# A block-inverse recurrence beside a gated network on one core: 16x16 diagonal blocks with one link, the visit of the values moved, two columns interleaved

## The chip, the cores and the metric

The kernel runs on one core of one Trainium2 chip. The metric is the device time of one execution in microseconds. The kernel before takes 1741.5 us (median of 3 runs, 1741.11 to 1744.32).

## The reference, cut to what matters

A block of a network for 4 sequences of 2048 tokens with 256 features, all in fp32. First an attention-like recurrence with 4 heads of 64, in chunks of 64 tokens, then a gated network of three hidden layers of 1024.

```python
h = layernorm(x) * (1 + ca) + sa
v = h @ Ww.T;  rk = unit(h per head);  wk = rk shifted by one token
A0 = -where(strict, (wk @ wk.T) * L, 0)          # 64x64 per chunk and head
A = inv(eye - A0)
intra = where(strict, (rk @ wk.T) * L, 0)
for each chunk:                                  # 32 in sequence
    v_new = A @ v - (A @ wk) @ S
    o = rk_g @ S + intra @ v_new
    S = gamma_C * S + wk_g @ v_new
x = x + ga * (h + (alpha * o) @ Wr.T)
h = layernorm(x) * (1 + cb) + sb
g = silu(h @ w1.T * s1) * (h @ w2.T * s2)        # 256 -> 1024, the gated layer, l1
g = gelu(g @ h1.T * s)                           # l2
g = gelu(g @ h2.T * s)                           # l3
x = x + gb * (g @ w3.T * s3)                     # y, the last layer
```

## The kernel before, in words

There are 32 steps, one for each chunk of 64 tokens of all 4 sequences. The hidden activations of the network lie with features on the partitions and 256 tokens as columns. Each is kept as two parts, `act_hi` (rounded to fp32r) and `act_lo` (the rest), so each product of a 128x128 weight block is two matmuls of 256 columns, about 114 ns each. A step has 8 columns of `l1` (8 matmuls each), of `l2` and of `l3` (16 each), and the last layer `y` (32).

The steps are woven. In pass n of the steady state (`mixed`) TensorE does, for step n-1, `l3` and `y`; for step n, `l1` and `l2`; between these columns stand the parts of the recurrence for step n, and, for step n+1 and n+2, what does not depend on the state (the letter `ahead` in the lists). The order is written out by hand in the lists `alone` (step 0), `opening` and `second` (step 1), `third` (step 2) and `mixed` (steps 3 to 33, 24 of them in a loop of two passes of 12). Every engine walks the same list in order and does its own share of each item (`part` in each engine's block), so an item's place fixes its place in five queues at once. There is no other planner.

The inverse of the 64x64 lower triangular matrix is built for 8 pairs of (half of the heads, q) in both halves of the partitions:

- `gram` gives the products; GpSimd masks them to `near` (inside a diagonal block of `SB`), `cross` (between such blocks inside a half of 32) and `far` (between the two halves).
- `fs` (VectorE, L921 to L939) is the forward substitution in all 8x8 diagonal blocks. `fs 0` reduces `near` to `low` and sets up `sub`; `fs 1` to `fs 3` do two rows each. A row is a shuffle, a product and a difference on 64 elements, each waiting for the one before.
- `expand` (L940) spreads `sub` to the block diagonal `inv` and transposes it.
- From 8 to 32 there are two links. The step matrix is cross times inverse (`first_term`, L1102; copied and transposed by `step_part`, L872); `square_and_term` (L1106) gives its square and its first term; `first_part` (L863) prepares both, and the third `n` part (L1334) multiplies them. ScalarE writes `diag` (L698).
- `lead` (L1359) works with the values: `own` applies the diagonal halves to the values, `old_state` reads the state, `inner` multiplies `far` and `diag`. `join` (L1338) adds the `corner` products. In the steady state `lead` also carries the `first_term` matmuls of the next step, and `join` its `square_and_term` matmuls; SP moves the transposed inverse between the halves of the partitions for that (`move_inverse`, L512).

In `mixed`, `lead` stands behind `l1` column 7, `join` behind `l2` column 2, the third `n` part and `state` behind `l2` column 4. The banks of the gated layer are `[mlp[0], mlp[1], solo[0]]`. In `l1` ScalarE makes `gate` and `act_hi`, VectorE the gated product `full` (L998), GpSimd `act_lo` (L652). In `l2` and `l3` ScalarE makes `full` and `act_hi`, VectorE `act_lo` (L879). VectorE also does the norms (`stats`, `norm`, `square`, `unit`), with two reciprocal roots on GpSimd (`stats`, `length`, L591).

Of the kernel before, what the change touches and what calls it, by code (L numbers as in the profile page):

```python
# [26 lines left out]
SB = 8  # L27
FS = SB - 1
MASKS = 3
PASS = 12  # L30
EPS = 1e-5
# [22 lines left out]
CO_N = CO_UNIT + HB  # L54
# [51 lines left out]
def main(nc, ctx, sb, sem, sems, x, wts, wv, wr, wmod, cT, scales, s3, decay, const, out):  # L106
# [39 lines left out]
    with ExitStack() as early:  # L146
# [55 lines left out]
    sub_row = sb("sub_row", [2 * NP, SB])  # L202
    sub_term = sb("sub_term", [2 * NP, SB])
    step_and_inv = sb("step_and_inv", [2, 2 * NP, HB])
    step_n, first_inv_t = (step_and_inv[:, i] for i in range(2))
# [3 lines left out]
    step_nt = sb("step_nt", [2 * NP, HB])  # L209
    square_t = sb("square_t", [2 * NP, HB])  # L210
    first_two = sb("first_two", [2 * NP, HB])
# [56 lines left out]
    def listed(first, columns, between):  # L268
# [28 lines left out]
        ("intra", 0), ("fs", 0), ("fs", 1), ("fs", 2), ("fs", 3), ("expand", 0), ("far", 0), ("stats", 0, 1), ("check", 2), ("n", 1),  # L297
        ("warm", WARM_LINK), ("n", 2), ("warm", WARM_LINK), ("n", 3), ("heads", 1), ("warm", WARM_LINK), ("norm", 0, 1), ("round", 0), ("square", 0, 1), ("length", 0, 1),
# [6 lines left out]
        ("norm2", 0), ("turn", 0), ("fs", 1), ("flag", 0), ("u", 0), ("flag", 1), ("ln2", 0), ("ln2", 1), ("parts", 0), ("residual", 0),  # L305
        ("round", 2), ("silu", 0))]
    second = listed([], layers[:2 * HK], {
        ("l1", 0): [("fs", 2, 0)],
        ("l1", 2): [("fs", 3, 0)],
        ("l1", 4): [("expand", 0, 0), ("far", 0, 0)],  # L310
        ("l1", 7): [("n", 1, 0), ("stats", 0, 1)],
        ("l2", 0): [("round", 3, 0), ("n", 2, 0), ("norm", 0, 1)],
        ("l2", 1): [("round", 4, 0), ("n", 3, 0), ("keys", 0, 0), ("square", 0, 1)],
# [16 lines left out]
        ("l3", 6): [("n", 1, 0), ("far", 0, 0), ("norm", 0, 1), ("residual", 0, 1), ("square", 0, 1)],  # L330
        ("l3", 7): [("parts", 0, 0), ("silu", 0, 0), ("length", 0, 1), ("n", 2, 0), ("y", 0, 0), ("unit", 0, 1), ("y", 1, 0), ("n", 3, 0)],
# [4 lines left out]
        ("l2", 1): [("solve", 1, 0), ("fs", 3, 1), ("expand", 0, 1), ("stats", 0, 2)],  # L336
        ("l2", 2): [("state", 0, 0), ("norm", 0, 2)],
        ("l2", 3): [("far", 0, 1), ("n", 1, 1), ("square", 0, 2)],
        ("l2", 4): [("length", 0, 2), ("attn_out", 0, 0), ("residual", 0, 2)],
        ("l2", 5): [("n", 2, 1), ("unit", 0, 2)],  # L340
        ("l2", 7): [("n", 3, 1)],
# [79 lines left out]
    gated = [mlp[0], mlp[1], solo[0]]  # L421
# [34 lines left out]
    with nc.Block() as block:  # L456
        @block.sync
        def _(sp):
# [53 lines left out]
            def move_inverse(a):  # L512

                sp.wait_ge(inv_t_ready, a + 1)
                for c in range(2):
                    sp.dma_start(first_inv_t[half(1 - c)], square_t[half(c)]).then_inc(inv_moved, 16)

# [13 lines left out]
            def step(general, n, g, items):  # L531
# [3 lines left out]
                if whole or 2 <= n <= STEPS + 1:  # L535
# [5 lines left out]
                    if items is mixed and (whole or n + 1 < STEPS):  # L541
                        move_inverse(n + 1)
# [46 lines left out]
        def _(pool):  # L589
# [17 lines left out]
            def step(n, g, items):  # L607
                def part(name, k, a, p):
# [52 lines left out]
                    if (name == "lead" or name == "solve" and k == 0) and items is not alone:  # L661
# [35 lines left out]
        def _(act):  # L697
            def block_diagonal(a):  # L698

                act.wait_ge(rest_full, a + 1)  # L700
# [4 lines left out]
                ins.then_inc(diag_ready, 1)  # L705

# [4 lines left out]
            def step(n, g, items):  # L711
                def part(name, k, a, p):
# [33 lines left out]
                    if name == "n" and k == 3:  # L746
                        block_diagonal(a)
                    if name == "lead" or name == "solve" and k == 0:
# [7 lines left out]
                    if name == "join" or name == "solve" and k == 1:  # L756
                        new_values(a)
# [59 lines left out]
        def _(dve):  # L817
# [45 lines left out]
            def first_part(a):  # L863
                dve.wait_ge(first_full, a + 1)
# [634 lines left out]
```

## Time and profile before

| | |
|---|---|
| time, median of 3 runs | 1741.5 us |
| the profiled execution, its own time | 1740.73 us |
| its span, first to last instruction | 1738.9 us |
| TensorE busy | 1709.6 us, 98% |
| VectorE busy | 1115.6 us, 64% |
| ScalarE busy | 965.3 us, 56% |
| GpSimd busy | 593.6 us, 34% |
| mean granted TensorE clock | 0.991 |

The busy time of an engine is the union of its instructions in the profile. Matmuls are pipelined: a record of a 256-column matmul lasts 0.28 us while the next one starts 0.114 us after it, so durations of matmuls are best read from one start to the next. Apart from the first slices all slices of the span show TensorE busy at 90% or more.

### The profile page before, as it was taken

The numbers are of one execution on the slowest core, as the hardware profiler recorded it, in microseconds if no ns is written. First come the engines' busy times: TensorE is split into PE (matmuls) and PEld (weight loads), VectorE is DVE, ScalarE is ACT, GpSimd is POOL, SyncE is SP. The second block draws the span as 40 slices with busy tenths as digits, with TensorE's granted clock in tenths as the row PEclk, the third lists the DMA queues.
The fourth block names the chain that finished last, engine by engine and source line by source line (L and its number), as shares of the span: only waits on it lengthen the run. The fifth ranks groups of instructions, "written<-read, shape, count | busy, mean of one in ns | idle before, by whom it ended". The sixth has DMA issues, their size and how long they took to land.

```text
span 1738.9 us, 60528 instructions
## 1 busy us (share of the span) xinstructions
PE 1709.6 (98%) x25488; PEld 1644.4 (95%) x25488; DVE 1115.6 (64%) x3041; ACT 965.3 (56%) x2249; POOL 593.6 (34%) x694
## 2 busy tenths in 40 slices
PE   8799999999999999999999999999999999999999
PEld 5699999999999999999999999999999999999998
DVE  5777666666676666676666676666666666666432
ACT  4664555555555555555555555555555555565554
POOL 3544333243333243333243333243333243243111
PEclk8799999999999999999999999999999999999999
DMA  8201000000000000000000000000000000000000
GB/s 284 76 14 33 12 23 23 18 20 14 22 23 24 19 19 14 21 23 24 17 21 16 19 23 24 17 20 19 16 23 23 19 19 20 15 23 17 8 3 12
DMA packets 37356, 47.08 MB, mean 27 GB/s; under 512 B 9236, under 2 KB 29336, under 8 KB 37080
## 3 DMA queue, kind: packets, MB, share of 16 engines
q1 hardware_dynamic: 35088, 40.75, 8.5%
q8 instruction: 206, 3.38, 0.8%
q10 hardware_dynamic: 1992, 2.38, 0.5%
q14 instruction: 70, 0.57, 0.1%
HBM read 22.53 MB, written 8.39 MB: 18 GB/s over the span
## 4 chain that ended last, share of the span: by engine, by line
PE 93%; DVE 2%; issue 1%; POOL 1%; ACT 0%; DVEq 0%; POOLq 0%
PE mlp L1147 64%; PE mlp L1219 6%; PE solo L1147 3%; PE duo L1415 3%; PE solo L1288 3%; PE solo L1120 2%; PE duo L1336 1%; PE duo L1113 1%; PE duo L1404 1%; PE duo L1108 1%; PE duo L1309 1%; PE solo L1424 1%; PE solo L1130 1%; PE duo L1406 1%; PE duo L1300 1%
## 5 line engine op out<-in xcount | busy, mean ns | idle before, releaser
L1147 PE MATMUL mlp<-act_hi,w_hi 128*128 128x256 f32 x4096 | 967.7, 282 | 1.1 <-POOL act_lo L652 0.6
L1147 PE MATMUL mlp<-act_lo,w_hi 128*128 128x256 f32 x4096 | 945.1, 277 | 0.2
L1147 PEld LDWEIGHTS mlp<-act_hi,w_hi 128*128 128x128 f32 x4096 | 769.8, 188 | 10.1 <-POOL act_lo L652 1.3
L1147 PEld LDWEIGHTS mlp<-act_lo,w_hi 128*128 128x128 f32 x4096 | 770.1, 188 | 1.5 <-issue 0.6
L789 ACT ACTIVATE full<-mlp,scale_sb 128x256 f32<-128x256 f32 x512 | 246.2, 481 | 553.6 <-PE mlp L1147 553.4
L879 DVE TENSOR_TENSOR act_lo<-full,act_hi 128x256 fp32r<-128x256 f32 x512 | 240.2, 469 | 322.6 <-ACT act_hi L790 320.5
L652 POOL TENSOR_TENSOR act_lo<-full,act_hi 128x256 fp32r<-128x256 f32 x256 | 186.6, 734 | 496.0 <-ACT act_hi L779 496.0
L790 ACT ACTIVATE act_hi<-mlp,scale_sb 128x256 fp32r<-128x256 f32 x512 | 243.4, 475 | 0.0
L1147 PE MATMUL mlp<-xh,w_hi 128*128 128x256 f32 x768 | 186.4, 283 | 3.0 <-issue 2.4
L1147 PE MATMUL mlp<-xl,w_hi 128*128 128x256 f32 x768 | 185.4, 281 | 0.0
L591 POOL TENSOR_TENSOR rstd<-ve,minus_half 128x2 f32<-128x2 f32 x64 | 49.0, 766 | 334.2 <-DVE ve L828 334.0
L998 DVE SCALAR_TENSOR_TENSOR full<-mlp,scale_sb,gate 128x256 f32<-128x256 f32 x192 | 92.8, 484 | 94.7 <-ACT gate L774 92.2
L1147 PEld LDWEIGHTS mlp<-xh,w_hi 128*128 128x128 f32 x768 | 146.3, 191 | 4.8 <-issue 3.9
L774 ACT ACTIVATE gate<-mlp,scale_sb 128x256 f32<-128x256 f32 x192 | 91.3, 476 | 102.2 <-PE mlp L1147 98.4
L1147 PEld LDWEIGHTS mlp<-xl,w_hi 128*128 128x128 f32 x768 | 146.4, 191 | 0.0
L1219 PE MATMUL mlp<-w_hi,act_hi 128*128 128x256 f32 x512 | 118.2, 277 | 0.0
L1219 PE MATMUL mlp<-w_hi,act_lo 128*128 128x256 f32 x512 | 118.1, 276 | 0.0
L591 POOL TENSOR_TENSOR rinv<-ssm,minus_half 128x8 f32<-128x8 f32 x32 | 52.8, 1651 | 183.7 <-DVE ssm L857 183.7
L779 ACT CAST act_hi<-full 128x256 fp32r<-128x256 f32 x256 | 101.8, 398 | 10.8 <-DVE full L998 10.8
L1219 PEld LDWEIGHTS mlp<-w_hi,act_hi 128*128 128x128 f32 x512 | 96.1, 188 | 0.1
L1219 PEld LDWEIGHTS mlp<-w_hi,act_lo 128*128 128x128 f32 x512 | 96.1, 188 | 0.0
L763 ACT ACTIVATE h<-solo,sbm,cb 128x64 f32<-128x64 f32 x256 | 84.1, 438 | 0.3 <-PE solo L1424 0.3
(179 smaller groups left out, 2675.8 us busy)
## 6 DMA issues: line engine op xcount, KB each, us to landing
w_raw<-in_wts SPq DMA_DIRECT2D x22, 512.0 KB, 5.1
kg<-r SPq DMA_DIRECT2D x64, 126.0 KB
xin<-in_x SPq DMA_DIRECT2D x62, 128.0 KB
out_y<-y SPq DMA_DIRECT2D x62, 128.0 KB, 2.5
step_and_inv<-square_t SPq DMA_DIRECT2D x56, 64.0 KB, 2.0
wmod_sb<-in_wmod ACTq DMA_DIRECT2D x1, 1024.0 KB, 9.5
kg<-last SPq DMA_DIRECT2D x64, 2.0 KB
last<-r SPq DMA_DIRECT2D x64, 2.0 KB, 1.7
```

The costliest lines, as they stand in the source:

```text
L591: pool.tensor_tensor(dst[:], src[:], minus_half[:, 0:src.shape[1]], ALU.pow).then_inc(done, 1)
L652: pool.tensor_tensor(act_lo[0][:, k, :], full[k % 3][:], act_hi[0][:, k, :].bitcast(F32), ALU.subtract).then_inc(l_ready[0], 1)
L763: ins = act.activation(h2[:].rearrange("p k b n -> p (k b n)")[:, cols], solo[1][:, cols], ACT.Identity, bias=sbm[:, k, b:b + 1], scale=cb ...
L774: act.activation(gate[k % 2][:], gated[k % 3][:, 0:TOK], ACT.Silu, scale=scale_sb[:, 0, k:k + 1]).then_inc(l_act[0], 1)
L779: act.copy(act_hi[0][:, j, :], full[j % 3][:]).then_inc(l1_hi, 1)
L789: act.activation(full[k % 2][:], mlp[k % 2][:, 0:TOK], ACT.Gelu, scale=s)
L790: act.activation(act_hi[layer % 2][:, k, :], mlp[k % 2][:, 0:TOK], ACT.Gelu, scale=s).then_inc(l_act[layer], 1)
L879: dve.tensor_tensor(act_lo[layer % 2][:, k, :], full[k % 2][:], act_hi[layer % 2][:, k, :].bitcast(F32), ALU.subtract).then_inc(l_ready[la ...
L998: dve.scalar_tensor_tensor(full[k % 3][:], up, s, gate[k % 2][:], ALU.mult, ALU.mult).then_inc(prod_ready, 1)
L1147: mm = pe.matmul(dst, *general_ops, start=is_first and i == 0, stop=is_last and i == 1)
L1219: mm = pe.matmul(mlp[k][:, 0:D], *ops, start=j == 0 and i == 0, stop=j == HK - 1 and i == 1)
L1288: mm = pe.matmul(solo[0][:, b * D:(b + 1) * D], hT[:, kt, b, :], wv_sb[:, kt, :], start=kt == 0, stop=kt == KT - 1)
```

## The change

1. Diagonal blocks of 16 in place of 8. The substitution has 15 rows in six parts (`FS_ROWS`). The shuffles of a part come first, then a product and a difference for each row; row j works on 8 x j elements.
2. From 16 to 32 there is one link. `first_term` (16 matmuls of 64x64 by 32) is a part of its own, `n 1`; VectorE subtracts it from the unit matrix (`one_less`), ScalarE widens that to 64 columns (`step_wide`), and `inverse_turned` (16 matmuls of 64x64 by 32), `n 2`, gives the inverse of the half. `square_and_term`, the third `n` part, `join`, `first_part` and the transfers of `move_inverse` are gone.
3. `lead` stands behind `y`, ahead of the gated layer. Its two results are copied by VectorE between the columns of `l1` (`own`, `mask`) in place of ScalarE. GpSimd's decay of the state keeps its place behind `l1` column 7 (`decay`).
4. The first two columns of `l2` are interleaved: seven products of column 0, three of column 1, the last of column 0, the rest of column 1. The banks of the gated layer are `[solo[0], mlp[1], mlp[0]]`.
5. The constant table is 26 columns longer; they are not used.

```diff
-SB = 8
+SB = 16
 FS = SB - 1
+FS_ROWS = {1: (15, 14), 2: (13, 12), 3: (11, 10), 4: (9, 8), 5: (7, 6, 5), 6: (4, 3, 2, 1)}
+FS_PARTS = len(FS_ROWS)
+BETWEEN = 3
...
-        ("l3", 6): [("ln2", 1, 0), ("expand", 0, 1)],
-        ("l3", 7): [("parts", 0, 0), ("silu", 0, 0), ("y", 0, 0), ("y", 1, 0)],
-        ("l1", 7): [("lead", 0, 0), ("far", 0, 1), ("stats", 0, 2)],
-        ("l2", 0): [("old", 0, 0), ("norm", 0, 2)],
-        ("l2", 1): [("keys", 0, 0)],
-        ("l2", 2): [("join", 0, 0), ("square", 0, 2)],
-        ("l2", 3): [("length", 0, 2)],
-        ("l2", 4): [("n", 3, 1), ("state", 0, 0)],
+        ("l3", 6): [("ln2", 1, 0), ("fs", 4, 1)],
+        ("l3", 7): [("parts", 0, 0), ("silu", 0, 0), ("y", 0, 0), ("y", 1, 0), ("lead", 0, 0)],
+        ("l1", 2): [("own", 0, 0)],
+        ("l1", 3): [("own", 1, 0)],
+        ("l1", 5): [("mask", 0, 0)],
+        ("l1", 7): [("decay", 0, 0), ("far", 0, 1), ("stats", 0, 2)],
+        ("l2", 0): [("old", 0, 0), ("norm", 0, 2), ("fs", 5, 1)],
+        ("l2", 1): [("keys", 0, 0), ("fs", 6, 1)],
+        ("l2", 2): [("solve", 1, 0), ("square", 0, 2)],
+        ("l2", 3): [("length", 0, 2), ("expand", 0, 1)],
+        ("l2", 4): [("state", 0, 0), ("n", 1, 1), ("step", 0, 1)],
         ("l2", 5): [("unit", 0, 2)],
-        ("l2", 6): [("attn_out", 0, 0), ("residual", 0, 2)],
+        ("l2", 6): [("attn_out", 0, 0), ("n", 2, 1), ("diag", 0, 1), ("residual", 0, 2)],
...
-    gated = [mlp[0], mlp[1], solo[0]]
+    gated = [solo[0], mlp[1], mlp[0]]
...
+            def widen(a):
+
+                act.wait_ge(step_ready, a + 1)
+                after(act, inverse_full, a)
+                for i in range(2):
+                    ins = act.activation(step_wide[:, :, HB * i:HB * (i + 1)], one_less[:], ACT.Copy, scale=con[:, CO_BLK + i:CO_BLK + i + 1])
+                ins.then_inc(wide_ready, 1)
...
+                        for j in FS_ROWS[k]:
+                            ins = dve.stream_shuffle(rows[j], low[:, :, 0:j], [i // SB * SB + j for i in range(HB)])
+                        ins.then_inc(rows_ready, 1)
+                        dve.wait_ge(rows_ready, FS_PARTS * a + k)
+                        for j in FS_ROWS[k]:
+                            term = sub_term[:, 0:2 * NP * j].rearrange("p (m n) -> p m n", n=j)
+                            dve.wait_ge(sub_ready, SB * a + SB - j)
+                            dve.tensor_tensor(term, rows[j], sub[:, :, j:j + 1].to_broadcast([P, 2 * NP, j]), ALU.mult).then_inc(term_ready, 1)
+                            dve.wait_ge(term_ready, FS * a + SB - j)
+                            dve.tensor_tensor(sub[:, :, 0:j], sub[:, :, 0:j], term, ALU.subtract).then_inc(sub_ready, 1)
...
+            def first_term(m, c):
+
+                return pe.matmul(of_head(duo[1][half(c), 1, 0:2 * NP * HB])[:, m, :], cross[half(c), m // NP, m % NP, :], inv[half(c), m, :], start=True, stop=True)
+
+            def inverse_turned(m, c):
+
+                return pe.matmul(of_head(duo[1][half(c), 1, 0:2 * NP * HB])[:, m, :], step_wide[half(c), m, :],
+                                 inv_t[half(c), m, :], start=True, stop=True)
...
+                                if i == 1:
+                                    pe.wait_ge(prod_ready, nth(m, HK - 1 if k else HK - 3))
...
+                    elif name == "l2" and k == 0:
+                        layer("l2", 0, range(HK - 1))
+                    elif name == "l2" and k == 1:
+
+                        layer("l2", 1, range(BETWEEN))
+                        layer("l2", 0, range(HK - 1, HK))
+                        layer("l2", 1, range(BETWEEN, HK))
```

In the lists of the first steps: `alone` and `opening` get the added `fs` parts and lose the third `n` part, `second` has `fs 3` to `fs 6` behind `l1` columns 0 to 3 (before `fs 2` and `fs 3` behind columns 0 and 2), and `third` has `fs 1` to `fs 6` behind `l3` columns 1 to 4 for its own step, and for the next step `fs 4` to `fs 6` with `expand` behind `l2` column 5, `n 1` behind column 6 and `n 2` behind column 7.

## Rows read from the trace of the kernel before

**Rows 1.** The page, part 1: busy us (share of the span) xinstructions of each engine.

```profile
PE 1709.6 (98%) x25488; PEld 1644.4 (95%) x25488; DVE 1115.6 (64%) x3041; ACT 965.3 (56%) x2249; POOL 593.6 (34%) x694
```

**Rows 2.** The page, part 4: the chain of waits, share of the span by engine.

```profile
PE 93%; DVE 2%; issue 1%; POOL 1%; ACT 0%; DVEq 0%; POOLq 0%
```

**Rows 3.** Busy time in one steady step; PE, PEld, DVE, ACT, POOL, clock, DMA.

```profile
853.23:905.03 51.80, 51.80 (x799) 50.30 (x797) 34.39 (x94) 29.01 (x71) 18.07 (x21) 1.00 0.07 18
```

**Rows 4.** Timeline of TensorE, one step: start us, us, engine, line, operation.

```profile
875.01 0.28 PE L1147 MATMUL mlp<-xl,w_hi 128*128 128x256 f32 x1
875.22 0.27 PE L1120 MATMUL solo<-v,diag 64*64 64x64 f32 x2
...
889.81 0.39 PE L1147 MATMUL mlp<-act_hi,w_hi 128*128 128x256 f32 x1
```

**Rows 5.** Timeline of TensorE: small matmuls alone on two quarters.

```profile
156.07 1.12 PE L1104 MATMUL duo<-inv,cross 64*64 64x32 f32 x32 [0.69 <-DVE state L970]
...
1653.44 1.07 PE L1113 MATMUL duo<-diag,far 64*64 64x32 f32 x32
1654.45 0.38 PE L1147 MATMUL mlp<-act_hi,w_hi 128*128 128x256 f32 x1
```

**Rows 6.** Timeline of TensorE: small matmuls on four quarters.

```profile
836.22 0.75 PE L1336 MATMUL duo<-first_two,square_t 32*32 32x32 f32 x64
836.91 0.69 PE L1404 MATMUL duo<-intra,vn 64*64 64x64 f32 x32
837.42 0.65 PE L1406 MATMUL duo<-vn,kg 64*64 64x64 f32 x32
```

**Rows 7.** Busy time of TensorE in two woven stretches: lead, join.

```profile
876.20:877.22 1.02, 1.02 (x78) 1.00 0.06 16
831.26:832.38 1.12, 1.12 (x98) 1.00 0.00 0
```

**Rows 8.** Timeline of GpSimd behind the gated layer.

```profile
876.17 1.42 POOL L652 TENSOR_TENSOR act_lo<-full,act_hi 128x256 fp32r<-128x256 f32 x2 [0.18 <-ACT act_hi L779]
877.55 1.04 POOL L664 TENSOR_TENSOR state<-state,chunk_decay 128x512 f32<-128x512 f32 x1
...
879.94 0.71 POOL L591 TENSOR_TENSOR rstd<-ve,minus_half 128x2 f32<-128x2 f32 x1
```

**Rows 9.** Timeline of VectorE: parts of l3 and l2.

```profile
865.83 0.42 DVE L990 CAST xh<-h 128x512 fp32r<-128x512 f32 x1
...
880.68 0.88 DVE L844 SCALAR_TENSOR_TENSOR h<-xin,mv,mods 128x256 f32<-128x256 f32 x2
...
882.39 0.42 DVE L879 TENSOR_TENSOR act_lo<-full,act_hi 128x256 fp32r<-128x256 f32 x1
882.73 0.69 DVE L907 TENSOR_TENSOR kg<-kg,tail_decay 128x512 f32<-128x512 f32 x1
...
885.20 0.68 DVE L853 TENSOR_TENSOR r<-h 128x512 f32<-128x512 f32 x1
```

**Rows 10.** Timeline of VectorE: small operations of the substitution.

```profile
857.78 0.18 DVE L928 TENSOR_TENSOR sub<-con,low 128x8 f32<-128x8 f32 x1
...
858.63 0.22 DVE L937 TENSOR_TENSOR sub_term<-sub_row,low 128x64 f32<-128x64 f32 x1
858.89 0.22 DVE L939 TENSOR_TENSOR sub<-sub,sub_term 128x64 f32<-128x64 f32 x1
```

**Rows 11.** Timeline of TensorE: n 1 and solve of step 0.

```profile
31.68 0.50 PE L1104 MATMUL duo<-inv,cross 64*64 64x32 f32 x11 [1.26 <-DVE inv L942]
...
38.18 0.33 PE L1120 MATMUL solo<-v,diag 64*64 64x64 f32 x4
```

**Rows 12.** Busy time of all engines in three stretches of the start.

```profile
67.32:78.35 11.03, 10.43 (x64) 10.10 (x64) 6.66 (x25) 5.11 (x13) 3.92 (x7) 0.74 0.01 4
125.50:130.93 5.43, 4.04 (x39) 3.87 (x34) 5.33 (x10) 1.42 (x2) 5.02 (x3) 1.00 0.08 24
62.00:70.00 8.00, 4.95 (x15) 3.21 (x16) 2.00 (x6) 3.99 (x10) 2.52 (x2) 0.54 0.02 6
```

More of the change, by code:

```diff
@@ L201, in main @@
     sub = sb("sub", [2 * NP, SB])
[L202 to L205, printed above, removed]
+    sub_rows = sb("sub_rows", [2 * NP * max(sum(rows) for rows in FS_ROWS.values())])
+    sub_term = sb("sub_term", [2 * NP * FS])
     inv = sb("inv", [2 * NP, HB])
@@ L660, in part @@
                         ins.then_inc(far_ready, 1)
-                    if (name == "lead" or name == "solve" and k == 0) and items is not alone:
+                    if (name == "decay" or name == "solve" and k == 0) and items is not alone:
                         pool.wait_ge(inter_full, a)
@@ L745, in part @@
                             act.copy(gram[:, e], grams(a, e)[:, :, 0:C]).then_inc(gram_ready[e], 1)
[L746 removed]
+                    if name == "step":
+                        widen(a)
+                    if name == "diag":
                         block_diagonal(a)
[L748 removed]
+                    if name == "solve" and k == 0:
                         act.wait_ge(own_full, now)
@@ L945, in part @@
                         dve.wait_ge(inv_ready, now)
[L947 to L949 removed]
+                        dve.transpose(inv_t[:].rearrange("p k n -> p (k n)"), inv[:].rearrange("p k n -> p (k n)")).then_inc(inv_t_ready, 1)
+                    if name == "step":
                         step_part(a)
[L951 to L956 removed]
+                    if name == "own":
+                        dve.wait_ge(own_full, now)
+                        ins = dve.tensor_copy(vn[:, NP // 2 * k:NP // 2 * (k + 1)].rearrange("p q e n -> p (q e n)"),
+                                              solo[1][:, NP // 2 * P * k:NP // 2 * P * (k + 1)])
+                        if k == 1:
+                            ins.then_inc(own_ready, 1)
+                    if name == "mask":
+                        dve.wait_ge(mi_full, now)
+                        dve.tensor_scalar(mi[:].rearrange("p k n -> p (k n)"), duo[0][:, 1, 2 * NP * HB:4 * NP * HB], -1.0, None, ALU.mult).then_inc(mi_ready, 1)
                     if name == "state":
@@ L1327, in part @@
-                        for m in range(2 * NP) if k == 1 else ():
-                            for c in range(2):
-                                mm = first_term(m, c, c)
-                        for e, q, c, i in quarters if k > 1 else ():
-                            rows, m = quarter(c, i), e * NP + q
-                            if k == 2:
-                                mm = square_and_term(m, rows)
-                            if k == 3:
-                                back = quarter(1 - c if items is mixed else c, i)
-                                mm = pe.matmul(of_head(duo[1][back, 1, 0:2 * NP * HB])[:, m, :], square_t[rows, m, :], first_two[rows, m, :], start=True, stop=True)
@@ L1359, in part @@
-                    if name == "lead" or name == "solve" and k == 0:
-                        with_next = name == "lead" and (not isinstance(n, int) or n + 1 < STEPS)
-                        pe.wait_ge(const_in, 16)
-                        if with_next:
-                            pe.wait_ge(cross_ready, n + 2)
-                            pe.wait_ge(inv_ready, n + 2)
+                            pe.wait_ge(wide_ready, now)
+                        for m in range(2 * NP):
+                            for c in range(2):
+                                if k == 1:
+                                    mm = first_term(m, c)
+                                if k == 2:
+                                    mm = inverse_turned(m, c)
@@ L1365, in part @@
+                        mm.then_inc({1: step_full, 2: inverse_full}[k], 1)
+                    if name == "lead" or name == "solve" and k == 0:
+                        pe.wait_ge(const_in, 16)
                         pe.wait_ge(far_ready, now)
```

190 lines of the change are left out of this document (64 added, 126 removed), and 9 rows, old and new, of the table third.

## The prediction

> **What bounds the kernel now.** I read the busy shares first: TensorE is busy 98% of the span, VectorE 64%, ScalarE 56%, GpSimd 34% [rows 1]. The chain of waits is 93% TensorE [rows 2]. So the kernel ends when TensorE's list of matmuls has been issued, and the only question in a steady step is how long that list is and whether a wait opens in it. One steady step is 51.8 us, with TensorE busy for all of it and VectorE for 34.39 [rows 3]. The timeline of TensorE then shows how little stands between the stages: the last gated (`l1`) matmul starts at 875.01, `lead` follows at 875.22, and the first matmul of `l2` column 5 starts at 889.81 without a wait before it [rows 4]. TensorE waits for nobody there, so VectorE and GpSimd have slack today; how much is read below.
>
> One thing matters more here than the count of matmuls. Small matmuls that alternate over only two quarters of the array cost twice as much each as those over four: 32 records of `inner` alone last from 1653.44 to 1654.45, 1.01 us (32 ns each); 32 of `first_term` alone are given 1.12, of which about 1.05 until the next matmul can start [rows 5]. (Each fp32 matmul stands as two records.) The 64 records of the third `n` part, on four quarters, take 0.69 (836.22 to 836.91, 11 ns each), and 32 of `state` on four quarters 0.51 (836.91 to 837.42, 16 ns each) [rows 6]. `inner` and `first_term` woven together, 64 records, last 1.02, hardly more than `inner` alone; `corner` woven with `square_and_term`, 98 records, last 1.12 [rows 7]. So today `first_term` and `square_and_term` are nearly free riders.
>
> **The change, part by part (one steady step).** All times are from one step, that of 853 to 905.
>
> TensorE, removed: `first_term` out of `lead` (1.02 becomes 1.01: 0.0), `square_and_term` out of `join` (1.12 becomes about 1.0, 32 records left on two quarters: -0.1), the third `n` part (-0.7). Added: `n` 1, 32 records alone on two quarters, 1.03, and `n` 2, `inverse_turned`, also 16 matmuls of 64x64 by 32 in two quarters, which the profile lacks. Its bounds are 0.5 (the 16 ns of `state`) and 1.1; the nearest row is `first_term` alone, same shape and same quarters, so 1.03. TensorE's own work thus grows by 1.03 + 1.03 - 0.8 = 1.25 us. `n` 1 stands beside `state` and `n` 2 beside `attn_out`, so no new change between large and small matmuls is paid.
>
> The move of `lead` from behind `l1` to ahead of it costs nothing by itself, but it uncovers the last gated columns. Counted from the last gated matmul (875.01), the low parts of columns 6 and 7 on GpSimd end at 876.17 + 0.73 = 876.9 and at 877.6 [rows 4, 8]. Today `lead` lies there until 877.2. With `l2` starting at once at 875.12 and 114 ns per matmul, product 6 of column 0 is due at 876.5 and waits 0.45; then three products of column 1 are put between, and product 7 is due at about 877.9, later than 877.6. The weaving hides column 7 and leaves 0.45 for column 6. At the front, `lead` needs in addition only `xh`, which VectorE has at 865.83 + 0.42 = 866.3 [rows 9], while the last layer's 32 matmuls keep TensorE 3.6 us behind `l3`, until 867.8: no wait. The two VectorE copies `own` and the `mask` op go between the gated products, whose distance is 0.9 for an op of 0.48: 0.9 - 0.4 leaves 0.5 for each 0.34. Hidden. ScalarE gives up two copies and gets two. SP's two transfers of `move_inverse` go; TensorE does not wait for them now (rows 4 have no wait), so 0.
>
> VectorE is where the step changes. The substitution goes from 6 rows to 15: 18 small ops become 45. Four batches stand in `l3` columns 3 to 6. A dependent op on 64 elements takes 0.22 and the next starts 0.26 later (858.63, 858.89); one on 8 elements takes 0.18 [rows 10]. The new ops have 8 to 120 elements; by these rows I take 0.15 + 1.05 ns per element, plus 0.035 to the next dependent one. Batches 1 to 4 then need 1.7, 1.6, 1.5 and 1.4 us beside an `act_lo` of 0.34 in columns of 1.83: a lag of some 0.2 us that has gone again at column 7. Hidden.
>
> Batches 5 and 6 and `expand` stand in `l2` columns 0, 1 and 3, and `n` 1, behind column 4, needs `expand`'s output. That chain has a fixed start: `norm` waits for `rstd`, which GpSimd gives at 879.94 + 0.71 = 880.65, because its queue holds the last two `act_lo`, `decay` (877.55) and two `far` before it, back to back; none of these moves against the gated layer's end [rows 8]. From `norm`'s first op at 880.68 [rows 9] VectorE must do, in order: `norm` 1.71 (880.68 to 882.39); batch 5 (rows of 7, 6, 5: three shuffles 0.55, six dependent ops of 0.24, less 0.1) 1.9; `act_lo` 0.34 (882.39 to 882.73); `keys` 0.6; batch 6 (four shuffles 0.6, eight ops of 0.21, less 0.1) 2.2; `act_lo` 0.34; `square` 0.68 + 0.69 + 0.17 with gaps, 1.6; `act_lo` 0.34; `expand`'s first op, of `act_lo`'s shape, 0.42 + 0.03. The sum is 9.5: `inv` is there at 890.15. TensorE would arrive at `n` 1 at 875.12 + 0.45 + 80 matmuls of `l2` (9.15) + `corner` with its change of mode 1.2 + `state` 1.15 = 887.1. So it waits about 3.1 us, and the 0.45 above is swallowed by this wait. The five ops of `first_part` and `step_part` that VectorE loses here (1.7 us) are already out of this sum.
>
> At this place the Trainium skill ("VectorE: DVE Perf Modes", § The TRN2 errata) gives a table with a cost of 58 cycles plus one per element, and beside it a measured fixed term of about 150. By the table the 21 ops of batches 5 and 6 would take an estimated 0.09 us each rather than 0.2, and the wait would be near 1 us instead of 3.1. The rows side with the second figure.
>
> Bounds of the two batches together (4.1): 3.5 if each op were as short as the 8-element one with its start to start at 0.2 and shuffles at 0.1; 5.5 if all 21 were at the 0.26 of 64 elements. The wait is then 2.5 to 4.5.
>
> **The sum.** Today `l2` column 5 starts at 889.81. Then: 890.15 + 0.05 + `n` 1 at 1.03 = 891.2, later by 1.4. `lead`, 1.99 us and 0.2 for its two changes between large and small matmuls, now lies ahead of `l1`: +2.2. `n` 2: +1.0. Per step 4.6, bounds 4.0 - 0.5 (`n` 2 on the low side) = 3.5 and 6.0. The same from the other side: work 1.25, wait 3.1, column 6 inside it, together 4.4. I take 4.6. Steps 3 to 30 have every item: 28 x 4.6 = 129.
>
> The start: in step 0 nothing else is behind the chain. 27 more small ops on VectorE are +4.4; between `n` 1 at 31.68 and `solve` at 38.18 there are 6.5 us today [rows 11], and 1.05 + 0.3 + 0.35 + 0.8 (two ScalarE copies) + 0.1 + 1.05 + 1.1 = 4.75 after: net +2.6. In step 1 eleven rows instead of four are put between the gated columns, where VectorE already holds TensorE up (64 matmuls in 11.03 us, clock 0.74) [rows 12]: +3.5. In step 2 two sets, one in `l3` and one in `l2`: TensorE waits today, 5.43 us for 32 matmuls of the last layer [rows 12], and VectorE gets some 9 us more; I take +5, between 1 and 10. Together +11, bounds 5 to 20.
>
> The profiled execution took 1740.73 (span 1738.9), 0.8 under the median of 1741.5. The sum 129 + 11 = 140 on the median gives 1881.
>
> **Rivals.**
> *A, VectorE's longer chain stays hidden* (the waits for `inv` never last). For it: VectorE is busy only 34 of 51.8 us. Against it: where it counts, between 880.68 and `n` 1, 9.5 us of work stand in 6.4. Its time: work 1.25 + column 6 at 0.45 = 1.7 per step, 48 in all, and 6 for the start: 1796.
> *B, the clock.* A wait of 3 us in each step lets TensorE fall to the lower level. In the start, a stretch of 8 us with TensorE busy for 4.95 ran at 0.54 of full clock; one with 4.04 of 5.43 busy stayed at 1.00 [rows 12]. If 10 us of each step ran at half speed, 5 us more: 1881 + 28 x 5 = 2021. The new step is busy 53 of 56, nearer to the second stretch. The Trainium skill ("TensorE: Matmul & The Clock Gate", Part 1) says that recent inactivity sets the engine to half rate; by that rule this wait would be at the edge.
> *C, faster or the same: the number of records is what costs.* 96 fewer records per step. If `n` 1 and `n` 2 ran at the 11 ns of the four-quarter rows, 0.34 each, they would be 0.1 cheaper than what they replace, and if in addition the chain of A were hidden and column 6 in time: 1741.5 - 28 x 0.1 + 3 at the start = 1742, no change that can be measured. It decides from `n` 1 lasting under 0.4 us; rows 5 speak against it with 1.0.
>
> **How the numbers follow.** Forecast 0.80 (own range 1835 to 1925), A 0.10, B 0.04, C 0.04, the rest unnamed. The range 1790 to 1915 takes in A and the bounds of the forecast. This measurement tells 0.2%, 3.5 us, from no change. Slower 0.95, same 0.02, faster 0.03.
>
> **What would show it.** The steady step in the profile after is 56.4 us. TensorE idles once in it, about 3 us, before the first `first_term` matmul, released by VectorE's `inv`; a wait of about 0.4 before product 6 of `l2` column 0, released by GpSimd's `act_lo`. `n` 1 and `n` 2 last 1.0 each. VectorE is busy without a gap from `norm` to `expand`. Granted clock near 0.99. I am wrong if `inv` is ready before 887.1 on this scale, if 32 records on two quarters take half of what rows 5 say, or if TensorE's large matmuls slow down.

## The result and the profile after

The changed kernel takes 1985.2 us (median of four runs, 1981.9 to 1988.2), against 1742.0 before: ratio 1.139, 95% interval 1.137 to 1.142. The forecast was 1881, with a range up to 1915. The direction was right, the size was not: +243 us (against the 1742.0 of this comparison) instead of +140.

The page of the changed kernel, parts 1 and 4 (beside [rows 1, 2]):

```profile
PE 1852.8 (94%) x22412; PEld 1774.2 (90%) x22412; DVE 1279.0 (65%) x4120; ACT 969.6 (49%) x2255; POOL 595.8 (30%) x694
...
PE 73%; DVE 13%; POOL 7%; issue 4%; ACT 1%; DMA 0%; DVEq 0%; ACTq 0%; POOLq 0%
```

TensorE has 3076 fewer records and yet 143 us more busy time. VectorE and GpSimd now hold 20% of the chain. Both things, slower work and a wait on the vector side, are to be found.

The waits of TensorE in the changed kernel (engine, its tile and line, what it waited for: us in total, times, longest):

```profile
PE duo L1110 <- DVE inv L946: 97.8, 30, 8.9
PE mlp L1153 <- POOL act_lo L650: 8.1, 31, 0.3
```

The first is the wait before `n 1`. Three of the 30 lie in the start, in steps 0, 1 and 2:

```profile
35.52 1.92 PE L1110 MATMUL duo<-inv,cross 64*64 64x32 f32 x32 [7.22 <-DVE inv L946]
128.95 1.12 PE L1110 MATMUL duo<-inv,cross 64*64 64x32 f32 x32 [3.07 <-DVE inv L946]
179.08 1.92 PE L1110 MATMUL duo<-inv,cross 64*64 64x32 f32 x32 [8.95 <-DVE inv L946]
```

Less these it is 78.6 over 27 steps, 2.9 each. The second is product 6 of `l2` column 0, 0.26 each. These are idle times by the profile, in which a matmul record lasts 0.28 us; start to start, product 6 comes 0.54 behind the matmul before it in place of 0.12 (1001.47 and 1002.01 below), so it costs 0.42.

Busy time in stretches of the changed kernel (start:end, us, then PE, PEld, DVE, ACT, POOL busy with instructions, granted clock, DMA share, GB/s): step 2 and two parts of it, then a steady step and four stretches of such steps.

```profile
133.06:205.37 72.31, 62.94 (x782) 60.02 (x781) 51.36 (x164) 32.30 (x77) 25.98 (x28) 0.92 0.07 20
170.00:179.05 9.05, 0.14 (x2) 0.00 (x0) 8.40 (x35) 0.84 (x2) 3.77 (x4) 0.78 0.19 58
179.05:190.00 10.95, 10.92 (x115) 10.62 (x116) 2.35 (x7) 3.90 (x9) 0.00 (x0) 0.72 0.01 2
...
987.00:1047.28 60.28, 57.18 (x700) 55.20 (x700) 39.52 (x129) 28.88 (x70) 18.16 (x21) 0.94 0.06 15
1011.97:1015.45 3.48, 0.65 (x46) 0.54 (x37) 3.26 (x11) 0.84 (x2) 0.73 (x1) 0.89 0.00 0
1015.45:1017.30 1.85, 1.85 (x33) 1.79 (x33) 1.83 (x4) 0.00 (x0) 1.01 (x1) 0.50 0.04 9
1017.30:1023.05 5.75, 5.75 (x34) 5.75 (x33) 1.45 (x3) 1.75 (x4) 0.00 (x0) 0.63 0.00 0
1035.89:1047.28 11.39, 11.39 (x99) 11.39 (x98) 8.65 (x38) 6.46 (x20) 2.83 (x4) 1.00 0.05 14
```

The steady step is 60.28 where it was 51.80 [rows 3]. (The mean of 24 steps, from one first matmul of `y` to the next, is 60.15 against 52.06; these means, "the period", are used below.) Three things stand in these rows. TensorE is busy for only 0.65 of the 3.48 us from 1011.97 to 1015.45. Behind that, `n 1` runs at a granted clock of 0.50 and the 5.75 us after it at 0.63. (Time at half rate, summed over the same 24 steps, is 5.55 us per step.) And 96 matmuls of `l3`, at full clock and without a wait, take 11.39 us, 118.6 ns each; before, the same 96 took 10.98, 114.4 each:

```profile
853.23:864.21 10.98, 10.98 (x100) 10.98 (x97) 8.49 (x36) 6.32 (x19) 2.81 (x4) 1.00 0.10 27
```

The mean pace of the large matmuls, which is given for each run below, is the mean time from one start to the next over the 24 steps, without the places where a wait, the lower clock or other work stands between (gaps over 125 ns).

The timeline of TensorE in that step (start us, us, engine, line, operation, idle before it and its releaser):

```profile
1001.47 0.28 PE L1153 MATMUL mlp<-act_lo,w_hi 128*128 128x256 f32 x1
1002.01 0.39 PE L1153 MATMUL mlp<-act_hi,w_hi 128*128 128x256 f32 x1 [0.26 <-POOL act_lo L650]
...
1011.24 0.28 PE L1153 MATMUL mlp<-act_lo,w_hi 128*128 128x256 f32 x1
1011.45 0.69 PE L1383 MATMUL duo<-intra,vn 64*64 64x64 f32 x32
1011.97 0.65 PE L1385 MATMUL duo<-vn,kg 64*64 64x64 f32 x32
1015.45 1.92 PE L1110 MATMUL duo<-inv,cross 64*64 64x32 f32 x32 [2.83 <-DVE inv L946]
1017.30 0.58 PE L1153 MATMUL mlp<-act_hi,w_hi 128*128 128x256 f32 x1
1017.68 0.41 PE L1153 MATMUL mlp<-act_lo,w_hi 128*128 128x256 f32 x1
1017.89 0.41 PE L1153 MATMUL mlp<-act_hi,w_hi 128*128 128x256 f32 x1
1018.10 0.41 PE L1153 MATMUL mlp<-act_lo,w_hi 128*128 128x256 f32 x1
```

Before the wait matmuls start some 118 ns apart, behind it 213 ns apart (1017.68 to 1018.32 in three). GpSimd and VectorE in the same step, to be laid beside [rows 8, 9]:

```profile
1005.00 0.89 POOL L589 TENSOR_TENSOR rstd<-ve,minus_half 128x2 f32<-128x2 f32 x1
```

```profile
1005.92 0.88 DVE L852 SCALAR_TENSOR_TENSOR h<-xin,mv,mods 128x256 f32<-128x256 f32 x2 [0.60 <-POOL rstd L589]
1007.65 0.21 DVE L935 STREAM_SHUFFLE sub_rows<-low 128x56 f32<-128x56 f32 x1
...
1009.57 0.42 DVE L879 TENSOR_TENSOR act_lo<-full,act_hi 128x256 fp32r<-128x256 f32 x1
...
1010.51 0.18 DVE L935 STREAM_SHUFFLE sub_rows<-low 128x32 f32<-128x32 f32 x1
...
1012.69 0.42 DVE L879 TENSOR_TENSOR act_lo<-full,act_hi 128x256 fp32r<-128x256 f32 x1
...
1014.88 0.42 DVE L946 TENSOR_TENSOR inv<-sub,con 128x256 f32<-128x256 f32 x1
```

`norm` starts when `rstd` is there and `inv` is written 9.4 us later (1005.92 to 1015.30). Batch 5 takes 1.92 (1007.65 to 1009.57), batch 6 takes 2.18 (1010.51 to 1012.69).

### The profile page after: what moved, and what is told of

Its sections match the earlier page's. It is cut to its first block, busy times and chain, and to the rows that moved or that the text cites. A ratio compares the mean times of both kernels' runs of the same rounds, so it can differ in the third digit from the quotient of the medians.

```text
span 1980.0 us, 56304 instructions
## 1 busy us (share of the span) xinstructions
PE 1852.8 (94%) x22412; PEld 1774.2 (90%) x22412; DVE 1279.0 (65%) x4120; ACT 969.6 (49%) x2255; POOL 595.8 (30%) x694
## 3 DMA queue, kind: packets, MB, share of 16 engines
q8 instruction: 182, 2.98, 0.6%
## 4 chain that ended last, share of the span: by engine, by line
PE 73%; DVE 13%; POOL 7%; issue 4%; ACT 1%; DMA 0%; DVEq 0%; ACTq 0%; POOLq 0%
PE mlp L1153 45%; PE mlp L1229 6%; PE solo L1153 5%; DVE sub_term L941 3%; PE duo L1394 3%; PE solo L1305 3%; PE duo L1110 3%; POOL act_lo L650 2%; DVE sub L943 2%; POOL far L601 2%; PE duo L1114 2%; DVE sub_rows L935 2%; PE duo L1119 1%; PE solo L1126 1%; DVE act_lo L879 1%
## 5 line engine op out<-in xcount | busy, mean ns | idle before, releaser
L1153 PE MATMUL mlp<-act_hi,w_hi 128*128 128x256 f32 x4096 | 1041.0, 293 | 8.6 <-POOL act_lo L650 8.1
L1153 PE MATMUL mlp<-act_lo,w_hi 128*128 128x256 f32 x4096 | 1017.0, 287 | 0.0
L1153 PEld LDWEIGHTS mlp<-act_hi,w_hi 128*128 128x128 f32 x4096 | 807.3, 197 | 21.7 <-POOL act_lo L650 14.4
L1153 PEld LDWEIGHTS mlp<-act_lo,w_hi 128*128 128x128 f32 x4096 | 807.4, 197 | 0.1
L1153 PE MATMUL mlp<-xh,w_hi 128*128 128x256 f32 x640 | 156.1, 281 | 2.0 <-DVE full L1004 2.0
L1110 PE MATMUL duo<-inv,cross 64*64 64x32 f32 x1024 | 52.4, 266 | 97.8 <-DVE inv L946 97.8
L1110 PEld LDWEIGHTS duo<-inv,cross 64*64 64x64 f32 x1024 | 49.2, 189 | 102.0 <-issue 101.9
L941 DVE TENSOR_TENSOR sub_term<-sub_rows,sub 128x120 f32<-128x120 f32 (+14 forms) x480 | 109.8, 229 | 31.2 <-issue 1.3
L943 DVE TENSOR_TENSOR sub<-sub,sub_term 128x120 f32<-128x120 f32 (+14 forms) x480 | 111.8, 233 | 17.4 <-DVE sub_term L941 1.0
L1229 PE MATMUL mlp<-w_hi,act_hi 128*128 128x256 f32 x512 | 119.9, 279 | 0.2 <-DVE act_lo L879 0.2
L782 ACT ACTIVATE gate<-solo,scale_sb 128x256 f32<-128x256 f32 x96 | 45.6, 476 | 144.7 <-PE solo L1153 144.4
```

Of the source, the lines that this page charges most:

```text
L941: dve.tensor_tensor(term, rows[j], sub[:, :, j:j + 1].to_broadcast([P, 2 * NP, j]), ALU.mult).then_inc(term_ready, 1)
L943: dve.tensor_tensor(sub[:, :, 0:j], sub[:, :, 0:j], term, ALU.subtract).then_inc(sub_ready, 1)
L1110: return pe.matmul(of_head(duo[1][half(c), 1, 0:2 * NP * HB])[:, m, :], cross[half(c), m // NP, m % NP, :], inv[half(c), m, :], start=True ...
L1153: mm = pe.matmul(dst, *general_ops, start=is_first and i == 0, stop=is_last and i == 1)
L1229: mm = pe.matmul(mlp[k][:, 0:D], *ops, start=j == 0 and i == 0, stop=j == HK - 1 and i == 1)
```

## The experiments

Theory: the wait of 3 us costs its own length and again through the clock; the rest is TensorE's own work and a slower pace of the large matmuls. Rivals: the clock follows the number or the kind of the small matmuls, not the wait; or the wait merely moves.

**n1_late: `n 1` and `n 2` later.** The same instructions, with `n 1` behind `l2` column 6 and `n 2` behind column 7.

```diff
-        ("l2", 4): [("state", 0, 0), ("n", 1, 1), ("step", 0, 1)],
+        ("l2", 4): [("state", 0, 0)],
-        ("l2", 6): [("attn_out", 0, 0), ("n", 2, 1), ("diag", 0, 1), ("residual", 0, 2)],
+        ("l2", 6): [("n", 1, 1), ("step", 0, 1), ("attn_out", 0, 0), ("residual", 0, 2)],
+        ("l2", 7): [("n", 2, 1), ("diag", 0, 1)],
```

> The changed kernel with n 1 and step ahead of attn_out behind l2 column 6 and n 2 and diag behind column 7, in place of columns 4 and 6, in the steady steps; nothing else. TensorE's matmuls are the same. Theory (the wait before n 1 costs its own 3.1 us and in addition about 3 us of a half-rate clock behind it): two columns, 3.7 us, now cover the wait, the clock stays at its upper level, and a steady step falls from 60.3 to about 54.2: 1985 - 28 x 6.1 = 1814, mean clock 0.99. Rival 1 (the half-rate stretches come from something else, the lighter work of TensorE for instance): only the wait goes, 1985 - 87 = 1898, mean clock 0.95. Rival 2 (VectorE's chain is only pushed on and something behind it waits instead): about 1985.

Measured: 1848.8 us, ratio to before 1.0625 (1.060 to 1.065), period 55.13. Its waits, then a step and its `n 1` (columns as above):

```profile
PE duo L1111 <- DVE inv L947: 19.2, 3, 8.9
```

```profile
1009.14:1010.19 1.05, 1.05 (x34) 1.01 (x33) 1.05 (x3) 0.84 (x2) 0.17 (x1) 1.00 0.00 0
...
1034.47:1089.60 55.13, 54.87 (x703) 52.96 (x702) 38.89 (x130) 29.11 (x71) 18.21 (x21) 1.00 0.06 17
```

The wait is left only in the start (3 times), and with it the lower clock: 1.00 over the whole step, `n 1` in 1.05. The pace of the large matmuls stays slow (mean 117.4 ns, before 114.4). So the wait brings the lower clock, and not the pace. The step is 5.02 shorter, where the theory expected 6.1: the wait was all of its 3, the clock gave back 2 and not 3. The step without wait and clock is still 3.07 above before, more than the 1.25 of own work that was forecast; what that is made of stands in the last part.

**fill: TensorE kept at work during the wait.** 26 large matmuls on a tile that nobody reads, ahead of `n 1`; their results are not used.

```diff
+                        if k == 1 and items is mixed:
+                            for _ in range(FILL):
+                                pe.matmul(duo[1][:, 1, 0:TOK], w_hi[:, BLK_H1, :], act_hi[0][:, 0, :], start=True, stop=True)
```

> The changed kernel with 26 more large matmuls (about 3.0 us, their result is not used) on TensorE just ahead of n 1 in each steady step, where it waits for inv. The time to n 1 is the same, but TensorE is busy in it. Theory (idle time drops the clock): the clock stays up, 3 us of each step come back, 1985 - 28 x 3 = 1900, mean clock 0.99. Rival (the low clock has another cause): same time as the changed kernel, 1985, mean clock 0.95.

Measured: 1934.3 us, 1.111 (1.109 to 1.113), period 58.11. The stretch of the fill, `n 1`, and the matmuls behind it:

```profile
1046.49:1049.75 3.26, 3.26 (x33) 3.12 (x26) 3.09 (x10) 0.84 (x2) 0.75 (x1) 1.00 0.02 5
1049.75:1050.80 1.05, 1.05 (x33) 1.01 (x32) 1.05 (x3) 0.00 (x0) 1.00 (x1) 1.00 0.00 0
1050.80:1054.68 3.88, 3.88 (x36) 3.88 (x33) 1.91 (x5) 1.75 (x4) 0.00 (x0) 1.00 0.00 0
```

`n 1` still begins only behind `inv`, yet the step is 2.04 shorter (60.15 to 58.11), since nothing behind it runs at half rate. The fill is a little longer than the wait: over 24 steps `n 1` begins 0.40 after `inv` is written, in the changed kernel 0.15. So 2.04 is a lower bound for the price of the clock, and 2.04 + 0.25 = 2.3 an estimate. Fill and n1_late differ by 58.11 - 55.13 = 2.98, which is the length of the fill. The expectation of 1900 took 3 for the clock, as in n1_late.

**fs5_early: a shorter wait.** Batch 5 moved ahead of `norm`.

```diff
-        ("l1", 7): [("decay", 0, 0), ("far", 0, 1), ("stats", 0, 2)],
-        ("l2", 0): [("old", 0, 0), ("norm", 0, 2), ("fs", 5, 1)],
+        ("l1", 7): [("decay", 0, 0), ("far", 0, 1), ("stats", 0, 2), ("fs", 5, 1)],
+        ("l2", 0): [("old", 0, 0), ("norm", 0, 2)],
```

> The changed kernel with substitution part 5 (1.9 us on VectorE) ahead of l2 column 0 in place of behind norm, into the time in which VectorE waits for ScalarE and for rstd. Theory: the wait before n 1 falls from 3.1 to about 1.2 us; if a wait so short leaves the clock up, a step falls by 4.9, to 1985 - 137 = 1848; if the clock still falls behind it, 1985 - 53 = 1932. Rival (the chain does not start at rstd, so the order does not matter): 1985.

Measured: 1877.7 us, 1.078 (1.076 to 1.080), period 56.31. Its wait:

```profile
PE duo L1110 <- DVE inv L946: 50.1, 30, 8.9
```

Without the start (6.8, 3.1 and 8.9) that is 31.3 over 27 steps, 1.16 each. The lower clock comes in 3 of 24 steps (0.57 us per step on average, in the changed kernel 5.55): one in which the wait is 3.29 and two in which it is 1.26. In the 24 of the 27 waits that last 0.97 to 1.19 it does not come. 56.31 is 1.18 above n1_late: a short wait costs about its length, and 1.7 us taken off the chain give 3.8 back.

**b_idle5: the wait without the change.** The kernel before, with five 512-element reductions on VectorE into an unused tile, and the last VectorE operation that `n` needs behind them.

```diff
+    scratch = sb("scratch", [IDLE])
...
-        ("l2", 3): [("length", 0, 2)],
+        ("l2", 3): [("length", 0, 2), ("late", 0, 1)],
...
+            def last_part(a, idle):
+                for i in range(idle):
+                    dve.tensor_reduce(scratch[:, i:i + 1], con[:, 0:512], AX.X, ALU.add)
```

> The kernel before, in which VectorE does five reductions of 512 elements (0.6 us each, result not used) behind l2 column 3 of each steady step and only then the last op of first_part, on which the third n part waits. TensorE so gets a wait of about 3.0 us in a step that has none, with nothing else of the change. Theory (such a wait costs itself and about as much again in the clock): 1742 + 28 x 6 = 1910, mean clock 0.95. Rival (the clock has nothing to do with the wait): 1742 + 84 = 1826, mean clock 0.99.

Measured: 1864.1 us, 1.068 (1.064 to 1.072), period 56.53. Its wait, then 6 us behind a wait in a step in which the clock falls, and a stretch with the wait in a step in which it stays up:

```profile
PE duo L1345 <- issue: 80.9, 28, 2.9
```

```profile
666.00:672.00 6.00, 6.00 (x154) 5.82 (x155) 1.49 (x4) 1.68 (x4) 0.00 (x0) 0.74 0.01 3
...
1002.90:1008.04 5.14, 2.22 (x20) 2.05 (x19) 4.57 (x10) 1.68 (x4) 1.64 (x1) 1.00 0.00 0
```

The profile names "issue" as what ended the wait; by VectorE's timeline the operation behind the reductions ends at 1007.94, 0.10 before TensorE goes on. The wait is 2.9, the same as in the changed kernel, and the step grows by 4.47, so about 1.5 comes on top. Half rate comes to 3.56 us per step on average, in one stretch each in 18 of 24 steps; in the changed kernel it comes in each of 24. Neither theory's number is hit: a wait of this length brings the lower clock in the old kernel too, but not each time. What decides it in a given step is open. The share of it differs from one execution to the next (1851.9 us at a mean clock of 0.978, 1865.2 at 0.966), and beside the wait stands other work: small matmuls before it in the changed kernel, large ones here. Neither was tried by itself. The pace stays at 114.7 ns, so it does not hang on waits or clock.

**b_unwoven: is the second of two woven groups free?** The kernel before, with `inner` and `first_term` one after the other.

> The kernel before, in which lead issues its 32 inner records first and then the 32 first_term records, in place of alternating them; the same instructions. Theory (32 records over two quarters of the array take 1.0 us whatever stands beside them, woven ones ride free): lead is longer by 1.0 us in each of 28 steps, 1741.2 + 28 = 1769. Rival (what costs is the number of records, and n 1 and n 2 of the changed kernel are dear for another reason): no change, 1741.

Measured: 1758.3 us, 1.0105 (1.009 to 1.012), period 52.61. The stretch that [rows 7] give as 1.02:

```profile
1042.24:1043.98 1.74, 1.74 (x78) 1.00 0.03 9
```

Taking two groups apart costs 0.7 in this stretch and 0.55 in the period, not the 1.0 of a group alone. Perhaps the second begins on quarters that the first leaves free; that is not shown. The premise on `first_term` holds in its direction.

**late_plain: the interleaving alone.** n1_late with `l2` columns 0 and 1 in their old order.

```diff
-                    if name in ("l1", "l3") or name == "l2" and (general or items is not mixed or k > 1):
+                    if name in ("l1", "l2", "l3"):
                         layer(name, k)
-                    elif name == "l2" and k == 0:
-                        layer("l2", 0, range(HK - 1))
-                    elif name == "l2" and k == 1:
-                        layer("l2", 1, range(BETWEEN))
-                        layer("l2", 0, range(HK - 1, HK))
-                        layer("l2", 1, range(BETWEEN, HK))
```

> The kernel n1_late without the interleaving of l2 columns 0 and 1: seven and one products of column 0 in a row, then column 1. Theory: with lead no longer behind l1, product 6 waits 0.4 us as before and product 7 waits another 0.45 to 0.5 for GpSimd's low part of gated column 7, as TensorE is the bound in this kernel: 1848.8 + 29 x 0.5 = 1863. Rival (the low part is there in time, the interleaving hides nothing): 1849.

Measured: 1858.9 us, 1.068 (1.066 to 1.070), period 55.53. Its waits for `act_lo`:

```profile
PE mlp L1154 <- POOL act_lo L651: 13.7, 61, 0.3
```

61 waits instead of 31. Interleaving hides column 7 and is worth 10 us, 0.4 per step.

**The pace, eight runs.** The first suspect was the longer constant table (`CO_N`, +26 columns). b_pad26, b_pad32, b_pad16 and b_pad64 lengthen it in the kernel before; b_sb16 lengthens only its buffer on the chip, b_dram16 only the table in memory.

```diff
-CO_N = CO_UNIT + HB
+CO_N = CO_UNIT + HB + 26
...
-    con = sb("con", [CO_N])
+    con = sb("con", [CO_N + 16])
...
-    c = np.zeros((P, CO_N), np.float32)
+    c = np.zeros((P, CO_N + 16), np.float32)
```

> The kernel before with the table of constants 26 columns longer, as in the changed kernel, so that all later buffers of a partition lie 104 bytes or so further on. In the trace large matmuls follow each other at one of two paces, 113.4 or 117.8 ns; at the slower one are 23% of them before and 85% after, about 1.0 us per step. Theory A (the place of the buffers sets the pace): mean pace rises from 114.4 to about 117, time 1741 + 30 = 1771. Theory B (the pace is set when a run of large matmuls begins behind small ones or a wait, by what stood there): no change, 1741.

> The kernel before with the table 32 columns (128 bytes a partition) longer. If buffers are put at multiples of 32 bytes, 26 columns (104 bytes) move what follows by 128 bytes too and this is the same layout as b_pad26: 1768, mean pace 117.2. If they are put back to back, 128 bytes is a rounder shift than 104, and the pace may stay at 114.4: 1742.

> The kernel before with the table 16 columns (64 bytes a partition) longer. If any shift of the buffers gives the slow pace (the kernel before sits at a lucky place): 1768. If only some shifts do: 1742.

> The kernel before with the table 64 columns (256 bytes a partition) longer, a round shift. If the pace depends on addresses within some round size that divides 256 bytes: 114.4 ns and 1741. If each shift gives another pace: 117 to 120, 1765 to 1795.

> The kernel before with the on-chip buffer of the table 16 columns wider, the table in memory as it was. If the place of the on-chip buffers sets the pace: as b_pad16, mean pace 119.9, 1794. If it is the table in memory (its rows, or what lies behind it): as before, 1741.

> The kernel before with the table in memory 16 columns wider, which no transfer reads, and the on-chip buffer as it was. The other half of b_sb16: if the place of the on-chip buffers sets the pace 1741 and 114.4 ns; if the table in memory does, 1794 and 119.9.

| kernel before with | us | ratio (95%) | mean ns per large matmul |
|---|---|---|---|
| +26 columns | 1767.7 | 1.0152 (1.013 to 1.017) | 117.2 |
| +32 | 1767.1 | 1.0148 (1.013 to 1.017) | 117.2 |
| +16 | 1793.6 | 1.0311 (1.029 to 1.033) | 119.9 |
| +64 | 1740.1 | 1.0001 (0.999 to 1.001) | 114.5 |
| +16, on-chip buffer only | 1794.9 | 1.0317 (1.030 to 1.034) | 119.9 |
| +16, memory only | 1740.0 | 0.9998 (0.999 to 1.001) | 114.4 |

The same 96 matmuls of `l3` in three of them (+26, +16 on the chip, +64):

```profile
1076.52:1087.92 11.40, 11.40 (x100) 11.40 (x99) 8.83 (x36) 6.46 (x20) 2.84 (x4) 1.00 0.09 27
```

```profile
1039.12:1050.71 11.59, 11.59 (x99) 11.59 (x98) 8.88 (x37) 6.56 (x20) 2.84 (x4) 1.00 0.08 22
```

```profile
1061.24:1072.22 10.98, 10.98 (x99) 10.98 (x98) 8.48 (x36) 6.32 (x19) 2.82 (x4) 1.00 0.09 27
```

In the second of them the place of the buffers behind the table is all that differs: 11.40, 11.59 and 10.98 us for the same work at full clock. 64 columns, 256 bytes, change nothing. +26 and +32 columns give the same time and pace, as they would if buffers were put at multiples of 32 bytes and both moved what follows by 128; where the buffers lie was not read out. In the changed kernel the pad was then taken out (a_pad0) or set to 16 (a_pad16):

```diff
-CO_N = CO_UNIT + HB + 26
+CO_N = CO_UNIT + HB
```

> The changed kernel with the table of constants as long as before (without the 26 unused columns). Theory A (the place of the buffers behind the table sets the pace of the large matmuls; 26 columns cost the kernel before 26 us and took its mean pace from 114.4 to 117.2 ns): mean pace 117.1 falls to about 114.5, 0.9 us per step, 1985 - 28 = 1957. Rival (in the changed kernel the slow pace comes from its own order of work): 1985.

> The changed kernel with 16 unused columns in place of 26. If a place is fast or slow by itself, it is the slowest as in the kernel before: mean pace about 120, 1985 + 20 = 2005. If place and program act together: anything from 114 to 120 ns, 1955 to 2005.

Measured: 1984.6 us, 1.141 (1.136 to 1.146), pace 118.1; and 1983.3, 1.140 (1.138 to 1.142), pace 116.9. Neither gives the 114.4 back, so both expectations of the theory fail. The pad by itself is thus not the cause in the changed kernel, though the same pad costs 26 us in the old one. Its other new buffers (`step_wide`, more rows of the substitution) move places too; none was moved alone. What slows its large matmuls stays open.

**late_nudge** (n1_late with the last transpose of each turn issued twice) asked whether the pace hangs on the order in which TensorE enters a stage.

> The kernel n1_late with the last of the four transposes of turn issued twice (0.1 us more in each step, the same result), just ahead of the longest run of large matmuls, l3 columns 2 to 7, which goes at 117.8 ns a matmul there and at 113.4 in the kernel before. Theory B (what stands just before a run sets its pace): the run may flip to 113.4, which gives 96 x 4.4 ns = 0.4 us per step back, 1849 - 28 x 0.3 = 1840. Theory A (place of the buffers): the pace stays, 1849 + 3 = 1852.

Measured: 1850.6 us, 1.064 (1.062 to 1.066), pace 117.4, as in n1_late: this one change of the order does not move it.

**late_early_pad0** joins n1_late, fs5_early and the pad taken out, as the best version that the runs so far pointed to.

> The changed kernel with all that the runs point to: n 1 and n 2 two columns later as in n1_late, substitution part 5 ahead of l2 column 0 as in fs5_early, and the table without the 26 columns. Theory: what is left over the kernel before is TensorE's own work, 1.25 us per step, 0.4 for product 6, and the start (18 us): 1742 + 28 x 1.65 + 20 = 1808. Rival (place of the buffers does not matter here): 1849.

Measured: 1855.2 us, 1.066 (1.064 to 1.068), period 55.30, pace 118.1. No better than n1_late, and far from the 1808 expected: n1_late has no wait in the steady steps that an earlier batch 5 could shorten, and the pace did not come back. No version with blocks of 16 comes near the kernel before.

## Why the prediction fell short

- **The wait before `n 1`, forecast 3.1: right.** It is 2.9 of idle time. Each term of its chain held: `norm` gated by `rstd`, batches at 1.92 and 2.18 (forecast 1.9 and 2.2), 9.4 from `norm` to `inv` (9.5).
- **TensorE's own work, forecast 1.25: right for the small groups, one change missed.** `n 1` at full clock is 1.05 (forecast 1.03). Counted from the first record of a group to the next large matmul, all small groups of a step together take 7.38 before and 8.49 in fill, +1.1. That small matmuls on two quarters are nearly free when woven is borne out by b_unwoven, with 0.7 rather than 1.0. But "no new change between large and small matmuls is paid" is wrong: a step has six in place of five, since `n 2` stands behind the large matmuls of `attn_out`. From the fifth last `attn_out` matmul to the second of `l3` it is 2.45, of which `n 2` is 1.05, against 1.20 before; the change costs 0.2:

```profile
784.07:786.52 2.45, 2.45 (x40) 1.00 0.00 0
785.24:786.29 1.05, 1.05 (x33) 1.00 0.00 0
```

```profile
685.39:686.59 1.20, 1.20 (x8) 1.00 0.05 14
```

- **Product 6 waits, column 7 does not: right,** at 0.42 start to start for the forecast 0.45. late_plain shows the hiding of column 7. The second way of the sum (work 1.25, wait 3.1, "column 6 inside it", 4.4) leaves it out by mistake: the 887.1 from which the wait is counted already holds the 0.45, so that way gives 4.8.
- **Batches 1 to 4, `own`, `mask` and `lead` ahead of `l1` hidden: right.** In `l3`, where the batches stand, TensorE is busy for all of 11.39 us, and the list of its waits has no wait that comes in each step but the two shown.
- **"Granted clock near 0.99": wrong, and the failed step.** It is 0.948. The forecast held rival B apart as an unlikely case, on the ground that a start stretch busy for 4.04 of 5.43 us stayed at 1.00 [rows 12] and the new step would be "nearer to" it. That compares shares of busy time of whole stretches. The longest single wait of that stretch is 1.39, half of the wait that was forecast:

```profile
130.93 0.74 PE L1336 MATMUL duo<-first_two,square_t 32*32 32x32 f32 x64 [1.39 <-DVE square_t L869]
```

  fs5_early, b_idle5 and the changed kernel agree that the length of the single wait matters: at 0.97 to 1.19 us the clock never falls, at 2.9 us in most steps of b_idle5 and in all of the changed kernel. The prediction had both parts in hand, a wait of 3.1 in each step and a mechanism for what follows it, and gave them 0.04 together. The rival's size was off the other way: 5 us per step were priced, 2.0 to 2.3 measured. 28 x 2.04 = 57 us; fill as a whole is 51 us faster than the changed kernel.
- **Large matmuls at their old pace: wrong.** Named as something that would refute, and given no price. 3 ns on some 340 large matmuls is 1.0 per step, 28 us. Its cause in the changed kernel is open.
- **The start, forecast 11 (5 to 20): 17.9.** The first `y` comes 7.6 later (6.1 forecast), step 2 is 72.31 against 62.00, +10.3 where 5 was taken between 1 and 10: `n 1` waits 8.9 there and 11 us at a clock of 0.72 follow.

Together, per steady step, in the mean of 24: wait 3.0 (start to start, less `state` itself), clock 2.3, small groups 1.1, pace 1.0, product 6 0.4, the sixth change 0.2: 8.0 of the 8.09 measured. Without clock and pace that is 4.7, where 4.6 was forecast. Over the 28 steps it is 7.95 each (222.5 us from the second `y` to the 30th); 222.5 + 17.9 + 0.7 at the end is the 241.1 by which the span grew. Rival A (chain hidden) and rival C (records count) are both refuted by the same row, the wait for `inv`, and C also by `n 1` at 1.05. The stated range ended at 1915 though the forecast's own range went to 1925; 1985 lies above both.

## What to carry to other kernels

When a step gets a wait on TensorE of the length of those here (some 3 us), price it twice: once by its length, and once by what runs at half rate behind it, and look at the length of the one wait rather than the busy share of a stretch. Useless matmuls put into such a wait bought back 51 us here, moving the waiting instruction by two columns 136 us. Before a change is judged to a few per cent, its pace per matmul is compared in a stretch that it doesn't touch: if that differs, a moved buffer may be mixed in with the change.

## What the runs showed of the hardware

- **The clock falls on one wait in an otherwise full stream.** With TensorE busy for 57.18 of 60.28 us, a wait of 2.83 is followed by `n 1` at 0.50 of the full clock, the lower of the two levels (1.2 GHz of 2.4), 1.85 us for what takes 1.05 at 1.00. It fell so in each of 24 steps; in b_idle5, behind waits of 2.9 as well, in 18 of 24, and in fs5_early behind none of 24 waits of 0.97 to 1.19. The Trainium skill ("TensorE: Matmul & The Clock Gate", Part 1) says that the clock has these two levels and that recent inactivity sets the lower one. By that rule, the trace agrees.
- **The place of on-chip buffers changes the pace of large matmuls.** In the kernel before, 96 matmuls of 256 columns take 10.98, 11.40 or 11.59 us (114.4, 118.8, 120.7 ns each) at full clock, with the table in front of the buffers 0, 104 or 64 bytes longer; with 256 bytes it is 10.98 again. The Trainium skill (the same page, "Wait — 56ns, not 53.3ns?") has columns divided by 2.4 GHz plus some 2.5 ns, an estimated 109.2 ns here; all the rows lie above it, and the measurement decides. Which buffer it is, and whether it is the operand that streams or the one that is loaded, wasn't tried and stays open.
